# A mixture of 32 experts: rows packed, packed blocks moving in both products, sums unpacked at the end

## The reference, cut to what matters

```python
h = concat([broadcast(cls_tok), h], axis=1)              # 64 x 26 x 192
h = h + L0_attn(layernorm(h))                            # causal: a row sees itself and the rows before it
x = layernorm(h)
gates = softmax(x @ gate_w + gate_b)                     # 32 gates a row
hid = gelu(einsum('btc,ech->bteh', x, w1) + b1)          # w1: 32 x 192 x 768, exact gelu
y = einsum('bteh,ehc->btec', hid, w2) + b2               # w2: 32 x 768 x 192
h = h + einsum('bte,btec->btc', gates, y)
```

## Time and profile before

| | us |
|---|---|
| median of 3 runs (2925.44 to 2933.19) | 2928.49 |
| the profiled execution, its own time | 2927.57 |
| its span, first to last instruction | 2925.8 |

### The profile page before, as it was taken

How to read it: one execution, slowest core, us unless ns; L and a number is a source line. 1 busy time by engine, 2 the same in 40 slices (tenths; PEclk the granted TensorE clock), 3 DMA queues, 4 the chain that set the end, 5 groups by cost and what they waited for, 6 DMA issues and landing times. The chain is left out here.

```text
span 2925.8 us, 61848 instructions
## 1 busy us (share of the span) xinstructions
PE 2689.8 (92%) x22697; PEld 2451.3 (84%) x22697; DVE 2051.2 (70%) x5175; ACT 1052.6 (36%) x2052; POOL 645.3 (22%) x816
## 2 busy tenths in 40 slices
PE   8889999999999999999999788799797889967778
PEld 7679999999999999999999677767466789956557
DVE  3867777776777777777777788723567676778877
ACT  2533333332333333323323444411355443324533
POOL 1312212122122122121221211021223201113561
PEclk9989999999999999999999899979898889978788
DMA  3101011011010010110100000057100100000000
GB/s 144 38 22 39 20 38 38 19 38 38 19 38 23 34 38 19 38 38 19 38 19 32 9 2 2 7 173 229 36 2 2 58 20 20 1 27 3 25 20 18
DMA packets 24481, 105.91 MB, mean 36 GB/s; under 512 B 4455, under 2 KB 9463, under 8 KB 19086
## 3 DMA queue, kind: packets, MB, share of 16 engines
q1 hardware_dynamic: 22654, 99.62, 9.9%
q0 software_dynamic: 1584, 3.30, 0.3%
HBM read 98.32 MB, written 6.64 MB: 36 GB/s over the span
## 5 line engine op out<-in xcount | busy, mean ns | idle before, releaser
L919 ACT ACTIVATE hid<-psum,dat 128x384 f32<-128x384 f32 (+1 forms) x912 | 554.2, 608 | 1144.1 <-PE psum L603 1029.9
L884 PE MATMUL psum<-w,hid_hi 128*128 128x384 f32 x2964 | 858.9, 361 | 2.2 <-DVE y_tok L935 1.6
L886 PE MATMUL psum<-w,hid_lo 128*128 128x192 f32 x2964 | 745.9, 252 | 0.0
L886 PEld LDWEIGHTS psum<-w,hid_lo 128*128 128x128 f32 x2964 | 571.0, 193 | 1.7
L884 PEld LDWEIGHTS psum<-w,hid_hi 128*128 128x128 f32 x2964 | 561.5, 189 | 5.5 <-issue 3.9
L953 DVE TENSOR_TENSOR hid_lo<-hid,hid_hi 128x384 fp32r<-128x384 f32 (+1 forms) x912 | 539.8, 592 | 31.5
L950 DVE CAST hid_hi<-hid 128x384 fp32r<-128x384 f32 (+1 forms) x912 | 340.7, 374 | 122.1 <-ACT hid L919 120.8
L976 DVE SCALAR_TENSOR_TENSOR h_tok<-psum,gate,h_tok 128x192 f32<-128x192 f32 x416 | 173.2, 416 | 248.0 <-PE psum L886 244.5
L603 PE MATMUL psum<-xa_hi,w_hi 128*128 128x384 f32 (+1 forms) x912 | 324.2, 356 | 1.6 <-ACT hid L919 0.5
L603 PE MATMUL psum<-xa_lo,w_hi 128*128 128x384 f32 (+1 forms) x912 | 322.4, 353 | 0.0
L603 PE MATMUL psum<-xb,w_lo 128*128 128x384 f32 (+1 forms) x912 | 321.8, 353 | 0.0
(11 more groups left out here) (367 smaller groups left out, 4213.8 us busy)
## 6 DMA issues: line engine op xcount, KB each, us to landing
raw<-in_L_exp SPq DMA_DIRECT2D x36, 1344.0 KB, 5.7
w_e<-in_L_exp SPq DMA_DIRECT2D x20, 576.0 KB, 4.0
w_e<-in_L_exp SPq DMA_DIRECT2D x20, 384.0 KB
pix<-in_pixels SPq DMA_DIRECT2D x6, 832.0 KB, 10.3
w_e<-in_L_exp SPq DMA_DIRECT2D x20, 195.0 KB
raw<-in_L_mlp SPq DMA_DIRECT2D x2, 1344.0 KB, 5.8
wp_raw<-in_L_att SPq DMA_DIRECT2D x1, 2304.0 KB, 8.3
route_rows<-in_rows_clear SPq DMA_DIRECT2D x1, 2000.0 KB, 22.9
```

The source lines that it names most:

```text
L884: nc.tensor.matmul(o[:, 0:2 * D], hid_hi[k % 2][:, m, c], w2[j][:, m, :], start=m == 0, stop=False)
L886: ins = nc.tensor.matmul(o[:, 0:D], hid_lo[k % 2][:, m, c], w2[j][:, m, 0:D], start=False, stop=m == HC - 1)
L919: nc.scalar.activation(hid[(6 * k + m) % 3][:, 0:128 * nt], bank[4 + (6 * k + m) % 4][:, 0:128 * nt], func, bias=bias).then_inc(s["h_act"] ...
```

## The change

The 64 equal class rows become one. `features_phase` and `gates` get `packed=True`: the copies that leave PSUM write the columns of `xa_hi`, `xa_lo` and `xb` in packed order, two columns with the class row and then 64 x 25 patch rows, 1602 in all; the four groups need three, three, three and two strided runs each where there was one. The gates are computed on packed rows. `turned_experts_phase` replaces `experts_phase` for the first layer: rows come in `SPANS` of 402, 400, 400 and 400 columns. `up` is as before on these. In `down` the second weights are stationary and the hidden blocks move: for a span, three products of 128 features (high by high, high by low, low by high) and two of a tile that holds the high weights of features 128 to 191 in its first 64 columns and their low weights in the others; the two halves are added at the very end, by a `fold` matrix of two identities. Sums are therefore features by rows. A gate now weights a column: SP writes the turned gates to DRAM and reads back, for each expert and span, one row onto all 128 partitions (`gate_b`), and DVE multiplies and adds (`y_new`, `y_sum`) where it had one combined operation. Second biases start `y_sum`. In the last expert the addition writes unpacked columns, PE turns them back to rows (`back`), DVE adds them to `h_tok` and takes the statistics (`add_back`). POOL's `split_turned` writes the second weights in two pieces for each part. The last two experts are written out and no longer in PE's loop. `CLOCK` keeps the width of an unrelated filler matmul at 428 columns.

```diff
...
+SPANS = [(0, 402), (402, 400), (802, 400), (1202, 400)]
+PACKED = 2 + IMG * (SLOT - 1)
+DONE = [(0, 3), (3, 3), (6, 3), (9, 4)]
...
+            def runs(i):
+
+                t0, n = TBLK[i]
+                a, e = 128 * t0, 128 * (t0 + n)
+                if not packed:
+                    return [(slice(a, e), lambda p: p)]
+                first, last, w = -(-a // SLOT), e // SLOT, SLOT - 1
+                out = []
+
+                def run(image, slot, end):
+                    x = 2 + w * image + slot - 1
+                    m = SLOT * image + slot - a
+                    out.append((slice(x, x + end - slot), lambda p: p[:, m:m + end - slot]))
+                if a == 0:
+                    out.append((slice(0, 2), lambda p: p[:, 0:1].to_broadcast([p.shape[0], 2])))
+                if a % SLOT:
+                    run(a // SLOT, max(a % SLOT, 1), SLOT)
+                out.append((slice(2 + w * first, 2 + w * last),
+                            lambda p: p[:, SLOT * first - a:SLOT * last - a].rearrange("p (m s) -> p m s", s=SLOT)[:, :, 1:SLOT]))
+                if e % SLOT > 1:
+                    run(last, 1, e % SLOT)
+                return out
...
+                                for x, of in runs(i):
+                                    p = of(src_p)
+                                    ins = nc.scalar.activation(like((xa_hi, xb)[part][:, x], p), p, ACT.Identity)
...
                         dve.wait_ge(s["hi_step"].sem, b["hi_step"] + i + 1)
-                    nc.vector.tensor_tensor(xa_lo[:, c], va, xa_hi[:, c].bitcast(F32), ALU.subtract)
-                    nc.vector.tensor_tensor(xb[64:128, c], vb, xb[64:128, c].bitcast(F32), ALU.subtract)\
-                        .then_inc(s["lo_full"].sem, 1)
+                    for x, of in runs(i) if packed else [(c, lambda p: p)]:
+                        qa, qb = of(va), of(vb)
+                        nc.vector.tensor_tensor(like(xa_lo[:, x], qa), qa, like(xa_hi[:, x].bitcast(F32), qa), ALU.subtract)
+                        ins = nc.vector.tensor_tensor(like(xb[64:128, x], qb), qb, like(xb[64:128, x].bitcast(F32), qb),
+                                                      ALU.subtract)
...
+        def split_turned(pool, b, e, j, i, before_low=None):
+
+
+            w_in, at = ((s["w_in0"], b["w_in0"]), (s["w_in1"], b["w_in1"]))[j]
+            pool.wait_ge(w_in.sem, at + 16 * (i + 1))
+            hold(pool)
+            r1 = raw[j][:, 0:2 * HID].rearrange("p (k n) -> p k n", k=2)
+            ra = raw[j][:, 2 * HID:2 * HID + HC * DA].rearrange("p (c n) -> p c n", c=HC)
+            rb = raw[j][:, 2 * HID + HC * DA:RAW].rearrange("p (c n) -> p c n", c=HC)
+            a_hi, a_lo, both = turned_w2(j)
+            nc.gpsimd.tensor_copy(w1_hi[j][:, :, :], r1).then_inc(s["w_split"].sem, 1)
+            nc.gpsimd.tensor_copy(a_hi, ra).then_inc(s["w_split"].sem, 1)
+            nc.gpsimd.tensor_copy(both[:, :, 0:DB], rb).then_inc(s["w_split"].sem, 1)
+            if before_low:
+                before_low()
+            pool.wait_ge(s["w_split"].sem, b["w_split"] + 6 * e + 1)
+            nc.gpsimd.tensor_tensor(w1_lo[j][:, :, :], r1, w1_hi[j][:, :, :].bitcast(F32),
+                                    ALU.subtract).then_inc(s["w_split"].sem, 1)
+            pool.wait_ge(s["w_split"].sem, b["w_split"] + 6 * e + 3)
+            nc.gpsimd.tensor_tensor(a_lo, ra, a_hi.bitcast(F32), ALU.subtract).then_inc(s["w_split"].sem, 1)
+            nc.gpsimd.tensor_tensor(both[:, :, DB:2 * DB], rb, both[:, :, 0:DB].bitcast(F32),
+                                    ALU.subtract).then_inc(s["w_split"].sem, 1)
...
+            def sync(sp):
+                def gate_rows(e, k):
+                    c0, n = SPANS[k]
+                    line = gates_d[e:e + 1, c0:c0 + n]
+                    sp.dma_start(gate_b[:, c0:c0 + n], bass.AP(line.tensor, line.offset, [[0, 128], [1, n]]))                        .then_inc(gate_in[k], 16)
+                sp.wait_ge(s["t_used"].sem, gating["kept"])
+                sp.dma_start(gates_d[:, :], gate_t[0:E, :]).then_inc(gate_out, 16)
+                sp.wait_ge(gate_out, 16)
+                for k in range(4):
+                    gate_rows(0, k)
+                for e in range(E):
+                    if e + 2 < E:
+                        sp.wait_ge(s["w_split"].sem, b["w_split"] + 6 * (e + 1))
+                        sp.dma_start(raw[e % 2][:, :], dram[e + 2]).then_inc(w_in[e % 2].sem, 16)
+                    for k in range(4):
+                        if e + 1 < E:
+                            sp.wait_ge(s["y_used"].sem, b["y_used"] + down_unit(e, k) + 2)
+                            gate_rows(e + 1, k)
+
+            def gpsimd(pool):
+                def next_weights(e, j, i):
+                    pool.wait_ge(s["h_split"].sem, b["h_split"] + 24 * e + 12)
+
+                    def before_low():
+                        pool.wait_ge(s["h_split"].sem, b["h_split"] + 24 * e + 24)
+                        hold(pool)
+                    split_turned(pool, b, e + 1, j, i, before_low)
+                next_weights(0, 1, 0)
+                with pool.Fori(0, E // 2 - 1) as i:
+                    for j in range(2):
+                        next_weights(2 * i + 1 + j, j, i + 1)
...
+                def second_biases():
+
+                    gating["tensor"][2](pe)
+                    x_made(pe, x_at, TOK)
+                    w = dat[0:E, DATA_COLS[b2_col]]
+                    for u in range(8):
+                        c0, n = SPANS[u // 2]
+                        if u >= 4:
+                            pe.wait_ge(s["y_used"].sem, b["y_used"] + u - 3)
+                        nc.tensor.matmul(bank[u % 4][:, 0:n], w[:, 128 * (u % 2):128 * (u % 2) + 128],
+                                         gate_t[0:E, c0:c0 + n], start=True, stop=True).then_inc(s["y_full"].sem, 1)
...
+                def down(e, j, k):
+
+                    n = SPANS[k][1]
+                    a_hi, a_lo, both = turned_w2(j)
+                    u = down_unit(e, k)
+                    pe.wait_ge(s["h_split"].sem, b["h_split"] + 24 * e + 6 * k + 6)
+                    for part in range(2):
+                        pe.wait_ge(s["y_used"].sem, b["y_used"] + u + part - 3)
+                        o = bank[(down_unit(0, k) + part if not is_last(e) else u + part) % 4][:, 0:n]
+                        for m in range(HC):
+                            hi, lo = hid_hi[k % 2][:, m, 0:n], hid_lo[k % 2][:, m, 0:n]
+                            steps = ((a_hi, hi), (a_hi, lo), (a_lo, hi)) if part == 0 else ((both, hi), (both, lo))
+                            for y, (w, x) in enumerate(steps):
+                                ins = nc.tensor.matmul(o, w[:, m, :], x, start=m == 0 and y == 0,
+                                                       stop=m == HC - 1 and y == len(steps) - 1)
+                        ins.then_inc(s["y_full"].sem, 1)
...
+                def back(k):
+
+                    t0, nt = DONE[k]
+                    pe.wait_ge(s["dve_step"].sem, b["dve_step"] + added(E - 1, k))
+                    for part in range(2):
+                        u = back_unit(k) + part
+                        pe.wait_ge(s["y_used"].sem, b["y_used"] + u - 3)
+                        for y, t in enumerate(range(t0 + 2 * part, min(t0 + 2 * part + 2, t0 + nt))):
+                            o, c = bank[u % 4][:, D * y:D * y + D], slice(128 * t, 128 * t + 128)
+                            nc.tensor.transpose(o[:, 0:DA], y_all[0][:, c], shp[:, SHAPE_COLS["ident"]])
+                            ins = nc.tensor.matmul(o[:, DA:D], y_all[1][:, c], shp[:, SHAPE_COLS["fold"]], start=True,
+                                                   stop=True)
+                        ins.then_inc(s["y_full"].sem, 1)
+
+                def body(e, j, i):
+                    pe.wait_ge(s["w_split"].sem, b["w_split"] + 6 * (e + 1) - (2 if is_first(e) else 0))
+                    up(e, j, 0)
+                    if is_first(e):
+                        gating["tensor"][1](pe)
+                    for k in range(1, 4):
+                        up(e, j, k)
+                        if is_first(e) and k == 1:
+                            second_biases()
+                            pe.wait_ge(s["w_split"].sem, b["w_split"] + 6)
+                        down(e, j, k - 1)
+                        if is_last(e) and k > 1:
+                            back(k - 2)
+                    down(e, j, 3)
+                    if is_last(e):
+                        back(2)
+                        back(3)
+                over_experts(pe, body, 1)
...
+                def keep_second_biases():
+                    for u in range(8):
+                        c0, n = SPANS[u // 2]
+                        dve.wait_ge(s["y_full"].sem, b["y_full"] + u + 1)
+                        nc.vector.tensor_copy(y_sum[u % 2][:, c0:c0 + n], bank[u % 4][:, 0:n]).then_inc(s["y_used"].sem, 1)
...
```

(63 more changed lines are left out.)

126 lines of the change are left out of this document (112 added, 14 removed).

## The result

The change makes the kernel faster: median 2891.86 us (2889.73 to 2895.6) against 2927.97 for the kernel before beside it, ratio 0.9877, 95% interval 0.9863 to 0.989. The forecast was 2901, range 2882 to 2922. The profiled execution took 2893.52 us, its span 2891.7, 34.1 less than before's. One of the repeats of the changed kernel in experiment 5 took 4994.4 us, where its other three took 2893 to 2899; the ratio there leaves it out.

The account below looks back on a forecast made before the run. PE's own rate was taken to bound the expert loop. Loop saving 34.2, less 1 (packing), 0 (biases) and 6.8 (tail), gives 26.4 us; 2927.57 - 26.4 = 2901 us, range 2882 to 2922.

Parts of the forecast that it names:

- The loop: 32 experts, PE-bound: 43.80 us an expert against 44.87, 1.07 saved each, 34.2 us in all.
- The one price of 0.1823: Expert loop: every 400 column matmul, up or down, takes 0.1823 us, scaled from 0.175 at 384 columns.
- rival (b): Expert loop: 0.175 us is a floor, so 400 columns cost 0.175 too; 90 us saved, 2845 us; chance 5%.
- 33 to 37: Expert loop: us saved between the two bounds on a 400 column matmul, 0.1823 and 0.1820 us.
- Covers: Expert loop: DVE, POOL, ACT and loads stay hidden behind PE; POOL's low parts by 2.3 us, DVE at down(3) by 3.6.
- the collision: Expert loop: gather(2)'s two DVE additions fall into POOL's low parts and make POOL late by about 1.2 us.
- Rival (a): Expert loop: POOL against DVE makes PE wait, deciding from 2.3 us late; about 3020 us if low parts double; chance 7%.
- Head: Before the loop: packing costs 1 us, gates through DRAM 0, second biases 0.
- Packing: Feature phase: 14 more short operations each on ACT and DVE, 0 to 2.5 us later; 1 us taken.
- Second biases: First expert: 16 matmuls of 400 columns replace 26 instructions; 0 us taken, bounds -2.7 and +2.6.
- Gates through DRAM: Before gather(0): gates go to DRAM and back by about 198, in time for the first down sum; cost 0.
- Tail: After the last expert: unpacking, turning back and statistics cost 6.8 us more, bounds 4 and 10.

Follow-up runs that it names:

- experiment 5: Changed kernel again, unchanged: ratio 0.9896; kernel before with the changed kernel's memory layout: 2928.1 us; kernel before with ten DVE copies ahead of the last mean: 2932.3 us.
- experiments 1 and 2: Changed kernel without packing, spans of 416 columns: 2945.84 us, ratio 1.0064; kernel before with up's last block at 450 columns, not 512: 2903.05 us, ratio 0.9916.
- experiment 3: Changed kernel with packed spans starting on multiples of 16 columns (0, 416, 816, 1216): 2890.93 us, ratio 0.9874.
- experiment 4: Changed kernel with one POOL low part done twice in each expert: the long one 2953.44 us, ratio 1.009; the short one 2907.52 us, ratio 0.9926.
- experiments 5 and 6: The second: changed kernel with thirteen DVE copies before the last four means, 2896.02 us; with seven PE filler matmuls behind the last turning back, 2896.99 us.
- experiment 7: Useless PE instructions added behind the last expert: 220 in the kernel before, 2932.19 us, ratio 1.0018; 36 in the changed kernel, 2898.51 us, ratio 0.9899.

## Why the prediction was right, step by step

**The loop: right, with two errors that cancel.** Predicted 43.80 an expert, measured 43.79; 1.09 saved where 1.07 was taken. The one price of 0.1823 is 0.1838 in up and on the average 0.181 in down: up takes 22.06 (21.9), down 21.73 (21.9). Per column 400, 416 and 450 cost 0.450 to 0.461 ns, against the 0.455 taken (experiments 1 and 2), so the price per column holds to 1.3%, and rival (b), the floor, is excluded; what two columns over 400 cost in down (experiment 3) shows that it isn't exact. The "33 to 37" between the two bounds doesn't follow from them: 0.1823 and 0.1820 give 34.2 to 36.6.

**Covers: right in sign, not in who pays.** POOL's end was to lie 2.3 us before the next expert, 1.1 with the collisions. It lies 2.0 before. The step put the collision on POOL, 1.2 us late. POOL's low parts take 6.6 us, and 6.2 in the first expert, where no addition falls beside them: POOL pays 0.4. DVE's two additions pay 1.82 + 1.38 - 2 x 0.57 = 2.1 us. DVE has the time. Rival (a) is real, and its threshold of about 2 us is what experiment 4 shows; with after's sizes it isn't reached.

**Head: small, as the sum had it.** Packing: DVE's last subtraction ends at 172.03 in place of 169.34, up(0) starts 1.7 later (176.16 in place of 174.47); 1 was taken, bounds 0 to 2.5. Second biases: 6.96 us from the first to down's first matmul in place of 8.12, -1.2 where 0 was taken, bounds -2.7 to +2.6; the 0.34 a matmul behind these bounds comes from no row, and PE's clock was granted 0.80 there. Gates through DRAM: written at 186.96, read from 189.29, needed at 204.09, where DVE waited for PE; cost 0, as said.

**Tail: right in size.** The last mean ends 6.4 us behind the last down matmul's start (about 7 said). From the end of the last expert's down(3), taken at the loop's period, to the next norm are 10.2 us (1367.62 - 31 x 43.787) in place of 4.0 (1395.18 - 31 x 44.877): 6.2 more, 6.8 predicted.

**What failed: the sum's silence on the later layers.** Head, loop and tail give 28.2 where 26.4 was said. The other 5.9 us, most of the 7.5 by which the profiled execution was under 2901, come from untouched code. The step that failed is an unwritten one, that code which isn't edited keeps its time; experiments 5 and 6 show that the 5.9 us are lasting. After's profile has 2.7 us less of waits for instructions there, but experiment 7 didn't move the whole stretch by moving them, so the cause of the 5.9 stays open. That the median came out inside the range is in part luck: 2891.86 lies at the lower end of the forecast's own bounds, 2892 to 2910, and the range reached down to 2882 for rival (b), which didn't happen.

## What to carry to other kernels

Before an operand is turned, count the columns that move in both forms: the turning alone lost 0.6% here, and only with the packing did the whole win 1.2%. Where PE is busy all the time, a matmul's price read from start times at two widths gave the new period within 0.1%, though by errors of about 0.7% in its halves that cancelled. Code that isn't edited took 5.9 us less here, lasting and only in part explained, so a total isn't explained until the untouched stretches are compared too.

## What was not expected of the hardware

- A DVE addition of two SBUF operands lasted 3.86 us beside a POOL instruction of 3.82, and 0.57 alone; POOL's own instruction of 3.50 lost 0.3. DVE's product with one operand in PSUM, started inside POOL's long part (at 313.48), lasted 0.58 all the same.
- PE waits of 0.5 to 2.2 us with no releaser in the next attention, which moved when 36 or 220 instructions were put ahead of them, and which all end 2.2 to 2.9 us after a transfer of instructions starts.
- PE at the upper level through the tail (transposes 0.11 us apart, not 0.21) brought the next layer nothing.
